# A planned GNN kernel: the end sums set in one series, new ranks for four kinds of work, and a row-wise tail for fourteen more blocks

## The reference, cut to what matters

```python
x = layernorm(x + L0(x, edge_attr, src, dst))
x = layernorm(x + L1(x, edge_index, edge_weight))
x = layernorm(x + L2(x, edge_index))
x = layernorm(x + L3(x, src, dst, edge_weight))
```

## Time and profile before

| what | us |
|---|---|
| median of 3 runs | 2836.69 |
| lowest and highest | 2823.86, 2838.3 |
| the profiled execution's own time | 2845.54 |
| span of the profiled execution | 2843.8 |
| TensorE busy | 1967.6 |
| VectorE busy | 1647.0 |
| ScalarE busy | 1503.0 |
| GpSimd busy | 1659.7 |

### The profile page before, as it was taken

How to read it: one execution, slowest core, us unless ns; L and a number is a source line. 1 busy time by engine, 2 the same in 40 slices (tenths; PEclk the granted TensorE clock), 3 DMA queues, 4 the chain that set the end, 5 groups by cost and what they waited for, 6 DMA issues and landing times. The chain is left out here.

```text
span 2843.8 us, 27560 instructions
## 1 busy us (share of the span) xinstructions
PE 1967.6 (69%) x8478; PEld 1007.7 (35%) x8478; DVE 1647.0 (58%) x3147; ACT 1503.0 (53%) x2238; POOL 1659.7 (58%) x1609
## 2 busy tenths in 40 slices
PE   6998787679988788899899879856888864000000
PEld 3444333226643333355444325544343343000000
DVE  4876799994888779735555431598565676000000
ACT  3787566565777678754777862434776622000000
POOL 6777777500027754000677757771777678777777
PEclk9999899889999889977999995665999955555555
DMA  3223222111668864102444490343111132000000
GB/s 63 70 65 81 54 59 68 44 38 65 190 120 47 49 50 41 51 17 62 128 136 138 128 229 22 93 118 97 55 59 51 57 114 85 15 16 20 22 21 21
DMA packets 219591, 203.19 MB, mean 71 GB/s; under 512 B 144815, under 2 KB 157958, under 8 KB 219446
## 3 DMA queue, kind: packets, MB, share of 16 engines
q1 hardware_dynamic: 164998, 154.80, 19.0%
q0 software_dynamic: 51200, 46.31, 12.5%
q10 hardware_dynamic: 3248, 0.34, 0.1%
HBM read 134.59 MB, written 80.28 MB: 76 GB/s over the span
## 5 line engine op out<-in xcount | busy, mean ns | idle before, releaser
L2318 POOL DMA_INDIRECT stab<-wk,rank_i x200 | 209.3, 1046 | 317.1 <-DVE wk L578 258.2
L535 ACT ACTIVATE b_s<-ps,vec 128x512 f32<-128x512 f32 (+1 forms) x370 | 250.5, 683 | 162.5 <-PE ps L529 63.3
L2315 POOL DMA_INDIRECT u<-x3tab,src_i x200 | 206.3, 1032 | 123.1 <-issue 61.5
L2315 POOL DMA_INDIRECT u<-x2tab,dpos_i x200 | 217.3, 1086 | 80.2 <-issue 75.4
L2315 POOL DMA_INDIRECT e_b<-x0tab,dpos_i x72 | 71.9, 998 | 313.8 <-DMA x0tab<-e_b 280.0
L2315 POOL DMA_INDIRECT u<-in_x_dram,src_i x200 | 201.4, 1007 | 76.6 <-issue 57.2
L2315 POOL DMA_INDIRECT u<-in_x_dram,dst_i x200 | 201.1, 1006 | 64.3 <-issue 59.8
L2318 POOL DMA_INDIRECT out_dram<-u,sfin_i x200 | 196.5, 982 | 66.4 <-issue 66.4
L2318 POOL DMA_INDIRECT out_dram<-u,dst_i x176 | 193.7, 1100 | 56.3 <-issue 56.3
L523 PE MATMUL ps<-b_h,blk_c 128*128 128x512 f32 (+1 forms) x296 | 173.0, 668 | 63.0 <-ACT b_gl L543 62.3
L614 PE MATMUL ps<-b_s,blk_j 128*128 128x512 f32 x296 | 184.9, 710 | 43.2 <-ACT b_s L656 29.0
(11 more groups left out here) (418 smaller groups left out, 4872.6 us busy)
## 6 DMA issues: line engine op xcount, KB each, us to landing
b_gl<-in_x_dram SPq DMA_DIRECT2D x98, 256.0 KB, 2.7
out_dram<-b_gl SPq DMA_DIRECT2D x98, 256.0 KB
wk<-dlist SPq DMA_DIRECT2D x50, 500.0 KB
wk<-slist SPq DMA_DIRECT2D x50, 500.0 KB
u<-stab SPq DMA_DIRECT2D x25, 510.0 KB
x2none<-b_gl SPq DMA_DIRECT2D x25, 250.0 KB
wk<-x2none SPq DMA_DIRECT2D x25, 240.0 KB
x2tab<-wk SPq DMA_DIRECT2D x25, 240.0 KB
```

The source lines that it names most:

```text
L535: return nc.scalar.activation(b_s[l][:, 0:w], pB[l][:, 0:w], ACT.Abs_reciprocal_sqrt, bias=col(EPSV))
L2315: pool.indirect_dma_start(out=o, out_offset=None, in_=tab, in_offset=at(ix), **kw).then_inc(s, 16)
L2318: pool.indirect_dma_start(out=tab, out_offset=at(ix), in_=a, in_offset=None, bounds_check=rows_n - 1, oob_is_err=False).then_inc(s, 16)
```

## The change

Five edits, all of them to what the planner is given; the functions that issue the instructions stay as they are. (1) In `ends_unit` a step `b1` to `b24` no longer follows its predecessor through the default but through a dependence with a delay of -.4 us. (2) `l0`, `l0d` and `xd1` get rank 1 in place of 2. (3) Dense blocks from 80 on get rank 1. (4) `BY_ROWS` is 60 in place of 74. (5) `HOLD` is empty.

```diff
-                prev = mark["<"][0].split(",") if mark["<"] else [steps[-1][0]] if steps else []
+                prev = [p for p in mark["<"][0].split(",") if p] if mark["<"] else [steps[-1][0]] if steps else []
...
-        BY_ROWS = 74
+        BY_ROWS = 60
...
-            unit(("l0", g), 2, "xt pe .68 +e0;xc act .6 -e0;et pe .4 +e0;ec act .3 -e0;f pe 2.05 +e1;fc act .6 -e1;fl dve .7;"
+            unit(("l0", g), 1, "xt pe .68 +e0;xc act .6 -e0;et pe .4 +e0;ec act .3 -e0;f pe 2.05 +e1;fc act .6 -e1;fl dve .7;"
...
-            unit(("l0d", g), 2, "a dve .7;b dve 1.41", [(("u2", g), "t", LANDED)] + ([(("l0d", g - 1), "b", 0)] if g else []))
+            unit(("l0d", g), 1, "a dve .7;b dve 1.41", [(("u2", g), "t", LANDED)] + ([(("l0d", g - 1), "b", 0)] if g else []))
...
-            unit(("lay", layer), 0, ";".join(f"b{g} pe {us}" + (" +e0" + both if g == 0 else "") for g in GROUPS) +
+            for g in range(1, NG):
+                deps[f"b{g}"] = list(deps.get(f"b{g}", ())) + [(("lay", layer), f"b{g - 1}", -.4)]
+            unit(("lay", layer), 0, ";".join(f"b{g} pe {us}" + (" +e0" + both if g == 0 else " <") for g in GROUPS) +
...
-            unit(("xd1", g), 2, "a dve 1.4;sq act .65;var dve .7;rs act .3;mul dve .7;dot dve 1.45",
+            unit(("xd1", g), 1, "a dve 1.4;sq act .65;var dve .7;rs act .3;mul dve .7;dot dve 1.45",
...
-            unit(("dense", n), 2, "t pe .68 +lane;u act|dve .7;c pe 1.13;sq act .6;j pe 1.13;r act 1.27;h dve 1.35;" + (ROW_MLP if n >= BY_ROWS else MLP),
+            unit(("dense", n), 1 if n >= 80 else 2, "t pe .68 +lane;u act|dve .7;c pe 1.13;sq act .6;j pe 1.13;r act 1.27;h dve 1.35;" + (ROW_MLP if n >= BY_ROWS else MLP),
...
-        HOLD = ((("lay", 1, "b10"), ("dst", 2, "t")),)
+        HOLD = ()
```

## The result

The changed kernel takes **2879.18 us** (median of 4 runs, 2863.92 to 2882.3) against 2830.28 (median of 4 runs, 2818.03 to 2838.3; the 2836.69 above is that of three of them) of the kernel before on the same chip: ratio **1.0148**, 95% interval 1.0103 to 1.0194. It is 1.5% slower, where 2792 (2738 to 2848) was forecast. The profiled execution has a span of 2876.8 us, 33 more than before.

The account below looks back on a forecast made before the run. Bound: a race of graph chain (ending 2264) and dense blocks (14 us later). Chain -106, dense -41 work, together -45 with idle: dense blocks bind; 2845.5 becomes 2800.5 profiled, 2792 us median, range 2738 to 2848.

Parts of the forecast that it names:

- the first rival: TensorE's clock stays up in the end-sum series, which then cost 20.5, 20.5 and 23 us: 2735 us, chance .12.
- the 106: Graph chain up to the last layer-3 gather: 10 + 42 + 24 + 30 = 106 us shorter, gathers ending at 2158.
- The norm's 42: Destination norm (xd1) before dense work: the second softmax starts sooner, taking 42 us off the chain.
- the third rival: Last stage bound by its three lanes, moved dense work costing 10.9 us a block there: slower, 2862 us, chance .15.
- the dense account: TensorE's work plus idle time up to the last dense step: -41 of work, together -45 us, ending about 2233.
- Layer 0's rank at 0: Layer-0 scores move forward by up to some 200 us beside gathers and sorting: 0 for the accounts.
- The series' dense pieces: Dense work moved out of the end sums of layers 0 to 2: +13, -6 and -22, sum -15 us on TensorE.
- Idle time -4: TensorE's idle part of the dense forecast: +15 (xd1), -7 (second softmax), -25 (layer-2 sums), +13 (layer 3's sums).
- The norm's +15 and -7: TensorE idle time: +15 us for dense work lost to xd1, -7 for the shorter wait for the second softmax.
- The term of +13 for layer 3's sums: TensorE account: +13 us because layer 3's sums now run beside the last dense blocks.
- The second rival: Idle time not filled: nothing more fits beside layer-2 sums (+25), xd1 takes its upper bound (+20): 2837 us, chance .16.
- The rival that the series stays broken: End sums still interrupted by other work, so only the shorter tails count: 2811 us, chance .05.

Follow-up runs that it names:

- rows63: The kernel before with only BY_ROWS changed, to 63 in place of 74: ratio 0.9913 to the kernel before.
- no_hold: The changed kernel, but with HOLD kept as in the kernel before: ratio 1.0129 to the kernel before.
- no_l0: The changed kernel, but with layer 0's scores (l0, l0d) back at rank 2: ratio 0.9955 to the kernel before.
- no_series: The changed kernel, but with the end sums broken by other work as before: ratio 1.0075 to the kernel before.
- no_xd1: The changed kernel, but with the destination rows' norm (xd1) back at rank 2: ratio 1.0061 to the kernel before.
- no_d80: The changed kernel, but with dense blocks 80 to 97 back at rank 2: ratio 1.0263 to the kernel before.
- only_l0: The kernel before with only layer 0's scores (l0, l0d) moved to rank 1: ratio 1.0298 to the kernel before.
- late_sums3: The changed kernel with layer 3's sums at rank 3 in place of 1: ratio 1.0186 to the kernel before.

## Why the prediction was wrong

**What held.** The series ran at half clock and took 38, 40 and 42 us (35, 42 and 45 forecast); nothing stood between their steps. The clock granted was 0.56, 0.54 and 0.51 in windows busy for 38.30 of 38.30, 40.20 of 40.20 and 42.23 of 42.30 us, so the first rival is out. The Trainium skill ("TensorE: Matmul & The Clock Gate", "Why this matters for your kernels") would have the clock full in a TensorE kept busy without gaps; these windows do not agree, and the measurement decides. The last dot came at 1154 (before 1165 forecast), and the last source score became the later of the two. The end was set by dense blocks, 129 us behind the chain on GpSimd (75 forecast). The tail took 22 to 31 full-clock us from the work, by the way of counting (26 forecast), and eleven blocks of it are worth 0.9% in rows63.

**The chain.** 62 us of the 106 came, counted at the first layer-3 gather (1931.33 against 1992.29, 61). Layer 0's 10 were lost: its series is 6.9 us shorter but begins 10.6 later. The norm's 42 came to 30 at the start of layer 1's series (1204.5 against 1234.3), because the source scores ended 19 us later, in a stage whose clock was 0.83 in place of 0.90. Layer 1's series gave 25.6 (24 forecast), layer 2's 48.6, of which its sums gave 20.7 back (210.1 in place of 189.4 us, VectorE busy for 180.8), so 28 for my 30. The stretch between them took 432.9 us in place of 411.6: 21 more, for which the sum had no term, only the third rival; no_hold shows where they come from, for with the hold kept it is 410 us again: the lanes taken just before the destination units.

**The step that failed** is the dense account: -45 forecast, +44 measured. Three terms of it, which overlap and do not add up, as each run takes one edit out of a whole order:

- *Layer 0's rank at 0 ("the work is the same and lies beside the gathers and the sorting").* It measured about 55 us (2322 against 2267 in no_l0). The work is the same, but its place was not: it left a stretch where TensorE had nothing better to do and pushed four dense blocks out of one where it had. The cover that I named for it was the cover that it gave to others.
- *The series' dense pieces "must be done elsewhere, and are done at 2.4 GHz there", for -15 in all.* It measured +27 (2322 against 2295 in no_series), +50 alone. Not all of the 64 us of pieces found idle time: 22 full-clock us of them (69 against 47) ended behind the last gather, where one takes 1/0.57 = 1.75 us, and alone 46 (48 against 2), where one takes 1/0.33 = 3 us. The +27 are little more than the spread between runs, the +50 are clear of it.
- *Idle time -4.* TensorE's idle time up to the last dense step rose from 388 to 415 us, +27: 20 in the first 653 us, 18 behind the last gather, and the 25 us that I wanted filled beside layer 2's sums were not (72.3 us idle before, 73.5 after). The norm's +15 and -7 came to some 25 us at the end (2322 against 2297 in no_xd1). The term of +13 for layer 3's sums was right, but only thanks to the late dense rank: up to the last dense step their products (L944, L962) keep TensorE busy for 13.7 us, 0.5 before, and 48.4 in no_d80.

I treated TensorE as one pot: work taken out of one place costs its own time in another. The runs show that the places have prices, and that the edits of the chain took their time out of stretches in which dense work had been running at little cost.

**The rivals.** The third came nearest, 2862 against 2879: it said that the moved work would go into the last stage and cost more there than where it had been, which is what happened. Its rate, 10.9 us a block, is about right beside the gathers (108 / 4 = 27 blocks in 272 us, 10.1) and too low behind them (69 / 875 of 98 blocks, 7.7, in 120 us, some 15). That its number came so near is partly luck, since layer 0's scores are not in it and the dense blocks lost 55 us to them. Its second half, a lane's stay of 33 us lost once nothing is held, was there, 24 us of chain in no_hold, but did not decide, since the chain was not the bound. The second rival, idle time not filled, was right in kind and ended at 2837, because it left the rate behind the last gather at one to one and layer 0's scores at nothing. The rival that the series stays broken is out, by the windows.

## What to carry to other kernels

Where filler work shares an engine with a chain, give each stretch a price, the time that one us of filler costs there, before anything is moved: a chain wait that is filled is not lost time, and shortening it pays only if the filler it held costs less at the end than the wait. A low-ranked piece of the chain may itself be the filler of a stretch that nothing else can use; raising its rank then costs, even if nothing waits for it. Undo the parts of a bundle one by one: here two of them, the series and the rank of layer 0's scores, cost more than the rest gained, and without them the bundle takes 2% off. Then try what is left as a whole, since in a planned order a part can change its sign with its company, as the norm's rank did.

## What was not expected of the hardware

TensorE's clock followed what was taken out: with layer 0's products gone from 300 to 546 us it was granted 0.82 in place of 0.91 (0.82 in only_l0 too, and 0.89 with the products back in no_l0), and dense blocks took 169.5 us for what had taken 154.7. TensorE was idle for 72 us of that stretch in place of 54. The order of late_sums3 is that of the changed kernel up to its last stage, yet it ran about 24 us later from 950 us on: ScalarE waited 10.2 and 8.1 us there for stores of a table (`x2none`), 4.6 and 3.1 in the changed kernel, and GpSimd stood still for 21.88 us before its next gather. Its four executions all took 2897 to 2903 us, but they come from another session than the changed kernel's, in which the kernel before itself ran from 2832 to 2871; whether program or session makes the difference is not shown. Single differences of some 20 us between the runs above are not to be read closely.
